# Zero-padded low keys for 128-row score products, and query and key weights split pair by pair on GpSimd

## The chip, the core and the metric

The kernel runs on one core of a Trainium2 chip. Its engines are TensorE (matmuls; loading weights is an instruction of its own beside them), VectorE, ScalarE, GpSimd and SyncE, which here issues the transfers (its queue is called SP). The metric is the time of one execution on the device in microseconds, less is better. Before the change it is 2414.99 us, the median of three runs (2414.29 to 2419.1).

## What is computed

A decoder layer on x of 8 sequences x 512 tokens x 512 features: self-attention with a router, cross-attention to a context of 77 tokens, and a feed-forward block over selected tokens. The change touches the self-attention alone, cut here to what matters:

```python
H, HD, W, G = 16, 64, 512, 128            # heads, head width, window, global tokens
h = rmsnorm(layernorm(x)) * norm_w        # (8, 512, 512)
q, k, v = (proj(w) for w in (w_q, w_k, w_v))   # each (8, 16, 512, 64)
ll = where(causal, q @ k.T * HD ** -0.5, NEG)
scores = h @ scorer_w + scorer_b          # a router: the 128 best tokens count twice
idx = top_k(scores, G)
lg = where(idx <= pos, q @ k[idx].T * HD ** -0.5, NEG)
attn = softmax(concat([ll, lg]))
o = attn[..., :W] @ v + attn[..., W:] @ v[idx]
return x + o @ w_out
```

As one window covers all 512 tokens, a selected token appears twice with the same score. The kernel therefore scores once, and counts the selected tokens' values twice.

## The kernel before

Matmuls run in a 32-bit type with rounded mantissa (F32R). To keep full precision each operand is split into a high part, rounded to that type, and a low part, the rest: a product is then high x high + low x high + high x low (`product`, three matmuls, L577 to L579). The weights of q, k and v lie in SBUF for the whole kernel, as `w_hi` and `w_lo`, each 128 x 4 x 1024. At the start they come in six pieces of 1024 KB (`W_ORDER`) through two halves of `o_t`: ScalarE rounds a piece (L368), VectorE subtracts (`split`, L477), and SP loads the next piece when a half is free.

A loop over the 8 sequences (`b`) does one batch after the other. Inside it the list `attention_plan()` sets the order, and each engine walks through the same list and does its own part: eight value projections ("v") with q and k of the first pair of heads among them, then 40 units ("s", 8 pairs x 5), then the last transposes and the output projection ("out"). A unit is one bank of 512 scores for one pair `p`, listed by `unit_blocks`: units 0 and 1 are one block of 512 keys (the last 128 queries of head 0 and of head 1), units 2 and 3 a block of 128 and one of 384, unit 4 two blocks of 256.

In step g TensorE makes the scores of unit g, the transposes of the probabilities of unit g-2 ("t", L673), the value products of unit g-3 ("pv", L688), and in units 0 and 2 the projection of q or k for the next pair ("q", "k", 12 matmuls). VectorE takes the maxima (L530, L525), copies the transposes to SBUF (L538), divides the outputs (L552, L553), and makes the low parts of q (L514) and k (L518). ScalarE makes the high parts (L392, L395, L396) and the exponentials (L405). The transposes of the outputs ("ot", L697) come at the end of a pair's unit 4, for the pair before. "t", "ot" and a few others take turns in two banks, `pt_bank`: each waits until the one before the last is copied out.

A score block is three matmuls into one bank: the high product over 128 rows (`q_both` holds 64 rows of high q and 64 of low q, `k_twice` the high k twice), the low product over 64 rows (high q x `k_lo`), and the causal mask in bf16 (`ident_b` x `causal_b`, L665):

```python
high = (q_both[:, p % 2, h, queries], k_twice[:, p % 2, h, 0:nk])
low = (q_both[rows, p % 2, h, queries], k_lo[rows, p % 2, 0:nk])
```

`rows` are the head's own 64 partitions. In unit 4 head 0 takes low first (L657, L659), and head 1 waits for that low product (`s_half`); elsewhere high comes first (L661, L664).

GpSimd makes the constants, the normalization of the next sequence in step 5 (`stats`, L325 to L339) and the residual of the output (L353). SP loads the next sequence at the start of a batch (L279) and moves the output's rows at its end (`results`).

Of the kernel before, what the change touches and what calls it, by code (L numbers as in the profile page):

```python
# [18 lines left out]
F32 = mybir.dt.float32  # L19
# [9 lines left out]
P = 128  # L29
# [97 lines left out]
def self_attention(nc, x, norm_w, w_q, w_k, w_v, w_out, scorer_w, scorer_b, x1):  # L127
# [3 lines left out]
    with ExitStack() as ctx:  # L131
# [9 lines left out]
        w_hi = {n: sb(f"w{n}_hi", [P, DC, H * HD], F32R) for n in "qkv"}  # L141
        w_lo = {n: sb(f"w{n}_lo", [P, DC, H * HD], F32R) for n in "qkv"}
# [7 lines left out]
        k_lo = sb("k_lo", [P, 2, S], F32R)  # L150
# [42 lines left out]
        s_ready, s_half = sem("s_ready"), sem("s_half")  # L193
# [10 lines left out]
        W_ORDER = [("v", 0), ("v", 1), ("q", 0), ("k", 0), ("q", 1), ("k", 1)]  # L204
        N_CONST = 9
# [41 lines left out]
        @block.sync  # L247
        def _(sp):
            sp.dma_start(xb[:, :, :], x_rows[0]).then_inc(x_in, 16)
            with nc.allow_non_contiguous_dma(reason="one column per chunk"):  # L250
                sp.dma_start(nw[:, :], norm_w.rearrange("(c p) -> p c", p=P)).then_inc(small_in, 16)
            sp.dma_start(sw[:, :], scorer_w.rearrange("d o -> o d").broadcast_to((P, D))).then_inc(small_in, 16)
            sp.dma_start(row_s[:, :], norm_w.rearrange("(o d) -> o d", o=1).broadcast_to((P, D))).then_inc(small_in, 16)
            sp.dma_start(sbias[:, :], scorer_b.rearrange("(o d) -> o d", o=1).broadcast_to((P, 1))
                         ).then_inc(small_in, 16)
            for i, (n, hw) in enumerate(W_ORDER):
                if i >= 2:
                    sp.wait_ge(split_lo, i - 1)
                sp.dma_start(o_t[:, DC * (i % 2):DC * (i % 2) + DC, :],
                             w_dram[n][:, :, 512 * hw:512 * hw + 512]).then_inc(w_loaded[i % 2], 16)  # L260
# [21 lines left out]
            sp.wait_ge(ht_lo_ready, DC * B)  # L282
            sp.dma_start(xb[:, :, :], x_rows[0]).then_inc(x_in, 16)
            results(B - 1)
            for half_done in x1_out:
                sp.wait_ge(half_done, 16 * B * TT // 2 + 1)

        @block.gpsimd
        def _(pl):
# [51 lines left out]

            stats(0)
            with pl.Fori(0, B) as b, done.loop(b, 14 + TT, B):
# [14 lines left out]
        def _(act):  # L358
# [6 lines left out]

            for i, (n, hw) in enumerate(W_ORDER):
                act.wait_ge(w_loaded[i % 2], 16 * (i // 2 + 1))
                nc.scalar.copy(w_hi[n][:, :, 512 * hw:512 * hw + 512],  # L368
                               o_t[:, DC * (i % 2):DC * (i % 2) + DC, :]).then_inc(split_hi, 1)
                if i == 1:  # L370
                    act.wait_ge(small_in, 64)
                    for c in range(DC):
                        normed(None, 0, c)
            act.wait_ge(split_lo, len(W_ORDER))
# [41 lines left out]
        def _(dv):  # L416
# [56 lines left out]
            def split(i):  # L473
                n, hw = W_ORDER[i]
                dv.wait_ge(split_hi, i + 1)
                cols = slice(512 * hw, 512 * hw + 512)
                nc.vector.tensor_tensor(w_lo[n][:, :, cols], o_t[:, DC * (i % 2):DC * (i % 2) + DC, :],  # L477
                                        w_hi[n][:, :, cols].bitcast(F32), ALU.subtract).then_inc(split_lo, 1)
# [14 lines left out]
            split(2)  # L493
            score_row(None, 0)
            split(3)
            for t in range(TT):
                rank(None, 0, t)
                if t in (1, 3):
                    split(4 + t // 2)
            with dv.Fori(0, B) as b, done.loop(b, 2 * TT + 2 * TT + 1 + NU, B):  # L500
                for kind, i in plan:
# [6 lines left out]
                    if kind in ("q_lo", "k_lo"):  # L508
                        slot, _ = pj(b, (kind[0], i))
                        dv.wait_ge(qk_hi, b * (2 * NPAIR) + 2 * i + (1 if kind == "q_lo" else 2))  # L510
                        for h in range(2):
# [5 lines left out]
                            else:  # L517
                                ins = nc.vector.tensor_tensor(k_lo[own, i % 2, :], pj_bank[slot][own, :],  # L518
# [55 lines left out]
        def _(pe):  # L574
# [46 lines left out]
            with pe.Fori(0, B) as b:  # L621
                for kind, i in plan:
                    if kind == "v":
# [7 lines left out]
                        for c in range(DC):  # L631
                            ins = product(pj_bank[slot][:, :], ht_hi[:, c, P * t:P * t + P], ht_lo[:, c, P * t:P * t + P],
                                          w_hi["v"][:, c, 512 * hw:512 * hw + 512],
                                          w_lo["v"][:, c, 512 * hw:512 * hw + 512], c == 0, c == DC - 1)
                        ins.then_inc(pj_ready, 1)
                    if kind in ("q", "k"):
                        slot, _ = pj(b, (kind, i))
                        pe.wait_ge(split_lo, 4 if i < NPAIR // 2 else 6)
                        pj_empty(b, (kind, i))
                        for c in range(DC):  # L640
                            ins = product(pj_bank[slot][:, :], w_hi[kind][:, c, P * i:P * i + P],
                                          w_lo[kind][:, c, P * i:P * i + P], ht_hi[:, c, :], ht_lo[:, c, :],
                                          c == 0, c == DC - 1)
                        ins.then_inc(pj_ready, 1)
                    if kind == "s":
# [6 lines left out]
                        for h, t, c0, nk in unit_blocks(u):  # L652
                            queries, rows = slice(P * t, P * t + P), head_rows(h)
                            high = (q_both[:, p % 2, h, queries], k_twice[:, p % 2, h, 0:nk])
                            low = (q_both[rows, p % 2, h, queries], k_lo[rows, p % 2, 0:nk])
                            if u == UNITS - 1 and h == 0:
                                nc.tensor.matmul(s_bank[slot][:, c0:c0 + nk], *low, start=True, stop=False  # L657
                                                 ).then_inc(s_half, 1)
                                nc.tensor.matmul(s_bank[slot][:, c0:c0 + nk], *high, start=False, stop=False)  # L659
                            else:  # L660
                                nc.tensor.matmul(s_bank[slot][:, c0:c0 + nk], *high, start=True, stop=False)  # L661
                                if u == UNITS - 1:
                                    pe.wait_ge(s_half, b * NPAIR + p + 1)
                                nc.tensor.matmul(s_bank[slot][:, c0:c0 + nk], *low, start=False, stop=False)  # L664
# [1097 lines left out]
```

## Time and profile before

| what | value |
|---|---|
| time, median of 3 runs | 2414.99 us |
| span of the profiled execution | 2414.0 us |
| self-attention, eight batches, one of them | 201.00 us |
| TensorE, VectorE, ScalarE, GpSimd busy in that batch | 197.31, 107.68, 71.46, 11.14 us |
| first stretch, to the first values | 48.70 us |
| cross-attention and feed-forward, from 1656 | 758.00 us |

The profile is of one execution; its span is the time from its first to its last recorded event, about 1 us less than the median of the runs. Times of matmuls overlap, since they are pipelined: the distance of two starts is the pace, not the duration that is printed. A granted clock of 1.00 stands for 2.4 GHz. "issue" as a releaser is time for which the profile shows no wait.

### The profile page before, as it was taken

How to read it: one execution, taken by the hardware profiler on the slowest of the kernel's cores; microseconds unless marked ns; L12 is line 12 of the kernel's file. 1: busy time of each engine (PE TensorE's matmuls, PEld its weight loads, DVE VectorE, ACT ScalarE, POOL GpSimd, SP SyncE). 2: the span in 40 equal slices, each digit the busy share in tenths (PEclk: the TensorE clock that was granted, in tenths of full speed). 3: DMA queues.
4: the chain of work that ended last, by engine and by line, in shares of the span. 5: the costliest groups of instructions: out<-in, count | busy, mean ns of one | idle time of the engine just before them, and what ended most of it. 6: DMA issues, size and time to landing. Idle time of an engine off the chain costs nothing. (4 is left out here: it accounts for less than half of the span.)

```text
span 2414.0 us, 35686 instructions
## 1 busy us (share of the span) xinstructions
PE 2241.6 (93%) x12029; PEld 1682.4 (70%) x12029; DVE 1349.6 (56%) x3145; ACT 845.5 (35%) x1541; POOL 429.2 (18%) x669
## 2 busy tenths in 40 slices
PE   3999999999999999999999999996898888878899
PEld 3786777678678677767767767773787888865543
DVE  4574376177257437617725743661787878845500
ACT  3442344144144234314414423441644444413210
POOL 2100000010010000001001000002866666620000
PEclk9999999999999999999999999997988888858999
DMA  5000000100100000010010000002013211141000
GB/s 183 1 1 31 23 1 10 45 1 1 54 1 1 31 23 1 10 45 1 1 54 1 1 28 27 1 10 91 29 56 102 83 55 55 53 152 50 1 0 18
DMA packets 46136, 80.23 MB, mean 33 GB/s; under 512 B 10067, under 2 KB 10067, under 8 KB 45448
## 3 DMA queue, kind: packets, MB, share of 16 engines
q1 hardware_dynamic: 45320, 75.85, 9.3%
q8 instruction: 103, 1.69, 0.3%
q0 software_dynamic: 640, 2.10, 0.2%
q14 instruction: 73, 0.60, 0.1%
HBM read 60.11 MB, written 17.83 MB: 32 GB/s over the span
## 5 line engine op out<-in xcount | busy, mean ns | idle before, releaser
L405 ACT ACTIVATE probs<-s_bank,nmax 128x512 f32<-128x512 f32 (+3 forms) x512 | 249.4, 525 | 421.6 <-DVE nmax L530 294.3
L530 DVE TENSOR_REDUCE nmax<-s_bank 128x1 f32<-128x512 f32 (+2 forms) x384 | 185.3, 510 | 305.7 <-PE s_bank L665 302.0
L688 PE MATMUL o_bank<-vals,probs_t 128*128 128x65 f32 x2560 | 322.2, 269 | 0.0
L688 PEld LDWEIGHTS o_bank<-vals,probs_t 128*128 128x128 f32 x2560 | 311.0, 192 | 1.4 <-DVE probs_t L538 1.4
L712 PE MATMUL pj_bank<-w_o,o_t 128*128 128x512 f32 x512 | 223.5, 597 | 6.0 <-ACT o_t L413 6.0
L538 DVE COPY probs_t<-pt_bank 128x512 f32<-128x512 f32 x320 | 218.0, 681 | 3.6 <-PE pt_bank L673 3.6
L319 POOL TENSOR_TENSOR idle<-ones 128x4 f32<-128x4 f32 x41 | 8.1, 198 | 1065.7 <-DMA probs<-in_x 1063.7
L673 PE MATMUL pt_bank<-ident,probs 128*128 128x128 f32 x1280 | 194.1, 274 | 0.0
L712 PEld LDWEIGHTS pj_bank<-w_o,o_t 128*128 128x128 f32 x512 | 97.2, 191 | 127.6 <-issue 127.6
L664 PE MATMUL s_bank<-k_lo,q_both 64*128 64x512 f32 (+3 forms) x448 | 184.9, 413 | 0.0
L514 DVE SCALAR_TENSOR_TENSOR q_both<-pj_bank,q_both 64x512 fp32r<-64x512 f32 x128 | 88.2, 689 | 141.6 <-ACT q_both L392 138.9
L661 PE MATMUL s_bank<-k_twice,q_both 128*128 128x512 f32 (+3 forms) x448 | 166.9, 373 | 0.0
L383 ACT ACTIVATE vals<-pj_bank,twice 128x512 f32<-128x512 f32 x64 | 43.9, 688 | 341.8 <-PE pj_bank L579 336.5
L1259 PEld LDWEIGHTS x_o_bank<-vx,p_t 77*128 77x128 f32 x1024 | 148.9, 224 | 17.2 <-issue 10.0
L1259 PE MATMUL x_o_bank<-vx,p_t 77*128 77x33 f32 x1024 | 143.8, 300 | 3.9 <-DVE att L1141 3.9
L570 DVE TENSOR_TENSOR probs<-pj_bank,probs 128x512 f32<-128x512 f32 x32 | 22.1, 692 | 213.8 <-PE pj_bank L712 195.3
L664 PEld LDWEIGHTS s_bank<-k_lo,q_both 64*128 64x128 f32 x448 | 81.9, 183 | 85.5 <-issue 72.1
L673 PEld LDWEIGHTS pt_bank<-ident,probs 128*128 128x128 f32 x1280 | 135.7, 141 | 0.0
L577 PE MATMUL pj_bank<-wv_hi,ht_hi 128*128 128x512 f32 x256 | 104.2, 407 | 22.9 <-ACT vals L383 9.9
L1245 PE MATMUL e_bank<-qk_bd,xl_t 128*128 128x308 f32 x256 | 96.9, 510 | 27.7 <-DVE e L1123 27.0
L1022 POOL TENSOR_TENSOR e<-e,fill 128x616 f32<-128x616 f32 x64 | 95.3, 1489 | 127.1 <-DVE fill L1129 126.9
L665 PE MATMUL s_bank<-causal_b,ident_b 128*128 128x128 bf16 x512 | 117.7, 230 | 0.0
(266 smaller groups left out, 4245.5 us busy)
## 6 DMA issues: line engine op xcount, KB each, us to landing
xb<-in_x SPq DMA_DIRECT2D x9, 1024.0 KB, 5.3
xt<-x SPq DMA_DIRECT2D x36, 256.0 KB, 2.8
probs<-in_x SPq DMA_DIRECT2D x32, 256.0 KB, 2.7
x<-probs SPq DMA_DIRECT2D x32, 256.0 KB, 2.0
am<-in_L_ffn_attention_mask SPq DMA_DIRECT2D x8, 1024.0 KB, 5.2
out<-x SPq DMA_DIRECT2D x32, 256.0 KB, 2.1
w_sb<-in_L_ffn_w SPq DMA_DIRECT2D x2, 4096.0 KB, 20.2
o_t<-in_L_attn_w_v SPq DMA_DIRECT2D x2, 1024.0 KB, 9.5
```

Source lines behind the costliest of these rows:

```text
L405: ins = nc.scalar.activation(probs[:, i % 2, c0:c0 + nk], s_bank[i % 2][:, c0:c0 + nk], ACT.Exp, bias=nmax[:, i % 4, n:n + 1])
L530: ins = nc.vector.tensor_reduce(nmax[:, i % 4, n:n + 1], s_bank[i % 2][:, c0:c0 + nk], AX.X, ALU.max, negate=True)
L538: nc.vector.tensor_copy(probs_t[:, i % 2, :], pt_bank[slot][:, :]).then_inc(ts_ready, 1)
L577: nc.tensor.matmul(out, lhs_hi, rhs_hi, start=start, stop=False)
L661: nc.tensor.matmul(s_bank[slot][:, c0:c0 + nk], *high, start=True, stop=False)
L664: nc.tensor.matmul(s_bank[slot][:, c0:c0 + nk], *low, start=False, stop=False)
L665: ins = nc.tensor.matmul(s_bank[slot][:, c0 + nk - P:c0 + nk], ident_b[:, :], causal_b[:, :], start=False, stop=True)
L673: ins = nc.tensor.transpose(pt_bank[slot][:, P * j:P * j + P], probs[:, i % 2, P * j:P * j + P], ident[:, :])
L688: ins = nc.tensor.matmul(o_bank[slot][:, o0:o0 + VW], probs_t[:, i % 2, c0 + P * kt:c0 + P * kt + P], vals[:, kt, 2 * p + h, :], start=(kt ...
L712: ins = nc.tensor.matmul(pj_bank[slot][:, :], o_t[:, c, P * i:P * i + P], w_o[:, c, :], start=(c == 0), stop=(c == NPAIR - 1))
L1245: ins = nc.tensor.matmul(e_bank[:, c, 0:CH * SK], xl_t[:, (i // 2) % 2, P * k:P * k + P], qk_bd[:, n.par, k].rearrange("p h k -> p (h k)") ...
L1259: ins = nc.tensor.matmul(o_bank[:, VX * h:VX * h + VX], p_t[:, i % 2, h // CH, P * (h % CH):P * (h % CH) + P], vx[:, n.par, 2 * CH * (i % ...
```

## The change

The low keys `k_lo` get a copy per head, in which the other head's 64 rows are zero; GpSimd writes the zeros once at the start. The low product then runs over all 128 rows with the same left operand as the high one: its low q meets zeros. The special order in unit 4 and its wait `s_half` go.

The weights of q and k are no longer kept. Per pair a slice of 128 columns of each is loaded (`w_raw`, 256 KB), GpSimd makes the high part by a multiplication by one and the low part by a subtraction (`split_slice`), after the projection that used the slice before is done, and the projection of the next pair waits for it (`w_made`). SP loads a slice when both splits of the one before are done (`next_slices`), ahead of the output's rows. The values' weights stay as they were. VectorE and ScalarE lose the four pieces of q and k at the start.

```diff
-        w_hi = {n: sb(f"w{n}_hi", [P, DC, H * HD], F32R) for n in "qkv"}
-        w_lo = {n: sb(f"w{n}_lo", [P, DC, H * HD], F32R) for n in "qkv"}
+        wv_hi, wv_lo = sb("wv_hi", [P, DC, H * HD], F32R), sb("wv_lo", [P, DC, H * HD], F32R)
+        w_raw = {n: sb(f"w{n}_raw", [P, DC, P]) for n in "qk"}
+        w_hi = {n: sb(f"w{n}_hi", [P, DC, P], F32R) for n in "qk"}
+        w_lo = {n: sb(f"w{n}_lo", [P, DC, P], F32R) for n in "qk"}
...
-        k_lo = sb("k_lo", [P, 2, S], F32R)
+        k_lo = sb("k_lo", [P, 2, 2, S], F32R)
...
+            def load_slices(i):
+                for n in "qk":
+                    sp.dma_start(w_raw[n][:, :, :], w_dram[n][:, :, P * i:P * i + P]).then_inc(raw_in[n], 16)
+            def next_slices(b):
+                for i in range(NPAIR):
+                    for n in "qk":
+                        sp.wait_ge(w_made[n], b * NPAIR + i + 1)
+                    load_slices((i + 1) % NPAIR)
+            load_slices(0)
...
             with sp.Fori(0, B - 1) as b:
+                sp.wait_ge(score_ready, b + 1)
                 sp.wait_ge(ht_lo_ready, b * DC + DC)
                 sp.dma_start(xb[:, :, :], x_rows[b + 1]).then_inc(x_in, 16)
+                next_slices(b)
                 results(b)
...
+            nc.gpsimd.memset(k_lo[:, :, :, :].bitcast(F32), 0.0).then_inc(const_made, 1)
...
+            def split_slice(n, count):
+                pl.wait_ge(raw_in[n], count * 16)
+                carry()
+                nc.gpsimd.tensor_scalar(w_hi[n][:, :, :], w_raw[n][:, :, :], 1.0, 1.0, ALU.mult, ALU.mult).then_inc(hi_made[n], 1)
+                pl.wait_ge(hi_made[n], count)
+                nc.gpsimd.tensor_tensor(w_lo[n][:, :, :], w_raw[n][:, :, :], w_hi[n][:, :, :].bitcast(F32),
+                                        ALU.subtract).then_inc(w_made[n], 1)
             stats(0)
+            for n in "qk":
+                split_slice(n, 1)
...
+                    if kind in ("q", "k"):
+                        pl.wait_ge(pj_ready, pj(b, (kind, i))[1])
+                        split_slice(kind, b * NPAIR + (i + 2))
...
-            split(2)
             score_row(None, 0)
-            split(3)
             for t in range(TT):
                 rank(None, 0, t)
-                if t in (1, 3):
-                    split(4 + t // 2)
...
-                                ins = nc.vector.tensor_tensor(k_lo[own, i % 2, :], pj_bank[slot][own, :],
+                                ins = nc.vector.tensor_tensor(k_lo[own, i % 2, h, :], pj_bank[slot][own, :],
...
-                        pe.wait_ge(split_lo, 4 if i < NPAIR // 2 else 6)
+                        pe.wait_ge(w_made[kind], b * NPAIR + i + 1)
...
-                            high = (q_both[:, p % 2, h, queries], k_twice[:, p % 2, h, 0:nk])
-                            low = (q_both[rows, p % 2, h, queries], k_lo[rows, p % 2, 0:nk])
-                            if u == UNITS - 1 and h == 0:
-                                nc.tensor.matmul(s_bank[slot][:, c0:c0 + nk], *low, start=True, stop=False
-                                                 ).then_inc(s_half, 1)
-                                nc.tensor.matmul(s_bank[slot][:, c0:c0 + nk], *high, start=False, stop=False)
...
+                            both = q_both[:, p % 2, h, P * t:P * t + P]
+                            nc.tensor.matmul(s_bank[slot][:, c0:c0 + nk], both, k_twice[:, p % 2, h, 0:nk],
+                                             start=True, stop=False)
+                            nc.tensor.matmul(s_bank[slot][:, c0:c0 + nk], both, k_lo[:, p % 2, h, 0:nk],
+                                             start=False, stop=False)
```

TensorE in unit 4 of the first pair, its order before (L657 and L664 are the low products, L659 and L661 the high ones):

```order
L657 MATMUL s_bank<-k_lo,q_both 128x256 [waits p_ready]
L659 MATMUL s_bank<-k_twice,q_both 128x256
L665 MATMUL s_bank<-causal_b,ident_b 128x128
L661 MATMUL s_bank<-k_twice,q_both 128x256
L664 MATMUL s_bank<-k_lo,q_both 128x256 [waits s_half]
L665 MATMUL s_bank<-causal_b,ident_b 128x128
L673 MATMUL pt_bank<-ident,probs 128x128 [waits ts_ready,p_ready]
```

The same place now (L681 is the high product, L683 the low one):

```order
L681 MATMUL s_bank<-k_twice,q_both 128x256 [waits p_ready]
L683 MATMUL s_bank<-k_lo,q_both 128x256
L685 MATMUL s_bank<-causal_b,ident_b 128x128
L681 MATMUL s_bank<-k_twice,q_both 128x256
L683 MATMUL s_bank<-k_lo,q_both 128x256
L685 MATMUL s_bank<-causal_b,ident_b 128x128
L693 MATMUL pt_bank<-ident,probs 128x128 [waits ts_ready,p_ready]
```

Head 0's two products have changed places, and no wait stands between the products any more; in the other units the order is what it was.

VectorE at the start, from the router scores to the factor of the values (`twice`), before:

```order
L440 TENSOR_SCALAR score<-score,sbias 128x4 [waits dve_step]
L477 TENSOR_TENSOR wq_lo<-o_t,wq_hi 128x4x512 [waits split_hi]
L446 COPY row_s<-pt_bank 128x512 [waits pt_ready]
L477 TENSOR_TENSOR wk_lo<-o_t,wk_hi 128x4x512 [waits split_hi]
L452 TENSOR_SCALAR junk,cnt<-row_s,score 128x512 [waits row_copied]
...
L463 TENSOR_SCALAR twice<-cnt 128x4 [waits dve_step]
L477 TENSOR_TENSOR wk_lo<-o_t,wk_hi 128x4x512 [waits split_hi]
```

And now:

```order
L473 TENSOR_SCALAR score<-score,sbias 128x4 [waits dve_step]
L479 COPY row_s<-pt_bank 128x512 [waits pt_ready]
L485 TENSOR_SCALAR junk,cnt<-row_s,score 128x512 [waits row_copied]
L488 SCALAR_TENSOR_TENSOR junk,cnt<-row_s,score,before 128x512 [waits dve_step]
L485 TENSOR_SCALAR junk,cnt<-row_s,score 128x512 [waits dve_step]
```

The subtractions for q and k are gone from VectorE (a third of the four stood among the rankings that are left out above). They stand on GpSimd now, in slices, behind the wait for the projection that used the slice before; this is the first of them in a batch:

```order
L363 ISA [waits pj_ready]
L338 TENSOR_TENSOR idle<-ones 128x4 [waits pool_step,raw_in_q]
L365 TENSOR_SCALAR wq_hi<-wq_raw 128x512
L367 TENSOR_TENSOR wq_lo<-wq_raw,wq_hi 128x512 [waits hi_made_q]
L382 REGISTER_ALU
```

## Rows read from the trace of the kernel before

**Rows 1.** A batch: stretch, length, busy PE PEld DVE ACT POOL, clock, DMA share, GB/s.
```profile
247.60:448.60 201.00, 197.31 (x1078) 146.98 (x1077) 107.68 (x254) 71.46 (x132) 11.14 (x26) 1.00 0.05 17
```

**Rows 2.** Timeline, TensorE, unit 1: start us, duration us, engine, line, operation, tiles.
```profile
384.53 0.39 PE L578 MATMUL pj_bank<-ht_hi,wq_lo 128*128 128x512 f32 x1
384.76 0.39 PE L579 MATMUL pj_bank<-ht_lo,wq_hi 128*128 128x512 f32 x1
384.98 0.39 PE L661 MATMUL s_bank<-k_twice,q_both 128*128 128x512 f32 x1
385.30 0.49 PE L664 MATMUL s_bank<-k_lo,q_both 64*128 64x512 f32 x1
385.73 0.23 PE L665 MATMUL s_bank<-causal_b,ident_b 128*128 128x128 bf16 x1
385.79 0.61 PE L673 MATMUL pt_bank<-ident,probs 128*128 128x128 f32 x4
```

**Rows 3.** Timeline, weight loads of the same unit; in brackets idle before and releaser.
```profile
384.76 0.19 PEld L661 LDWEIGHTS s_bank<-k_twice,q_both 128*128 128x128 f32 x1
385.30 0.18 PEld L664 LDWEIGHTS s_bank<-k_lo,q_both 64*128 64x128 f32 x1 [0.35 <-issue]
```

**Rows 4.** Timeline, TensorE, units 3 and 4, and the next pair's unit 3.
```profile
374.48 0.22 PE L661 MATMUL s_bank<-k_twice,q_both 128*128 128x128 f32 x1
...
375.71 0.61 PE L673 MATMUL pt_bank<-ident,probs 128*128 128x128 f32 x4
376.15 1.00 PE L688 MATMUL o_bank<-vals,probs_t 128*128 128x65 f32 x8
377.08 0.38 PE L657 MATMUL s_bank<-k_lo,q_both 64*128 64x256 f32 x1
377.39 0.39 PE L659 MATMUL s_bank<-k_twice,q_both 128*128 128x256 f32 x1
377.62 0.23 PE L665 MATMUL s_bank<-causal_b,ident_b 128*128 128x128 bf16 x1
...
378.33 0.61 PE L673 MATMUL pt_bank<-ident,probs 128*128 128x128 f32 x4
...
392.46 0.22 PE L661 MATMUL s_bank<-k_twice,q_both 128*128 128x128 f32 x1
```

**Rows 5.** Timeline, VectorE, ScalarE and TensorE from unit 3 to its transposes.
```profile
375.91 0.76 DVE L530 TENSOR_REDUCE nmax<-s_bank 128x1 f32<-128x128 f32 x2 [1.47 <-PE s_bank L665]
...
376.45 0.58 ACT L396 CAST k_twice<-pj_bank 64x512 fp32r<-64x512 f32 x1
...
377.62 1.38 DVE L518 TENSOR_TENSOR k_lo<-pj_bank,k_twice 64x512 fp32r<-64x512 f32 x2
...
379.04 0.69 DVE L525 TENSOR_REDUCE nmax<-s_bank 128x2 f32<-128x512 f32 x1
...
379.64 0.68 DVE L538 COPY probs_t<-pt_bank 128x512 f32<-128x512 f32 x1
...
380.88 0.60 PE L673 MATMUL pt_bank<-ident,probs 128*128 128x128 f32 x4
```

**Rows 6.** Timeline of the start: VectorE's last subtraction, TensorE's next value projection.
```profile
46.17 2.28 DVE L477 TENSOR_TENSOR wk_lo<-o_t,wk_hi 128x2048 fp32r<-128x2048 f32 x1
...
49.46 0.79 PE L577 MATMUL pj_bank<-wv_hi,ht_hi 128*128 128x512 f32 x1 [9.91 <-ACT vals L383]
...
50.05 0.63 PE L578 MATMUL pj_bank<-wv_hi,ht_lo 128*128 128x512 f32 x1
...
50.48 0.63 PE L579 MATMUL pj_bank<-wv_lo,ht_hi 128*128 128x512 f32 x1
```

**Rows 7.** GpSimd: L339 alone (count, ns min/median/max), and a subtraction's group (count, busy, mean ns).
```profile
L339 POOL TENSOR_SCALAR xb<-xb,st x36: 756/769/2797, 16.7 to 1510.2; 128x512 f32<-128x512 f32 x36
...
L1022 POOL TENSOR_TENSOR e<-e,fill 128x616 f32<-128x616 f32 x64 | 95.3, 1489 | 127.1 <-DVE fill L1129 126.9
```

**Rows 8.** Page, transfers by tile: count, KB each, median us to landing.
```profile
xb<-in_x SPq DMA_DIRECT2D x9, 1024.0 KB, 5.3
```

More of the change, by code:

```diff
@@ L192, in self_attention @@
         v_ready, v_sum_ready, qk_hi, qk_lo = sem("v_ready"), sem("v_sum_ready"), sem("qk_hi"), sem("qk_lo")
-        s_ready, s_half = sem("s_ready"), sem("s_half")
+        s_ready = sem("s_ready")
+        raw_in, hi_made, w_made = ({n: sem(f"{what}_{n}") for n in "qk"} for what in ("raw_in", "hi_made", "w_made"))
         max_ready, p_ready = sem("max_ready"), sem("p_ready")
@@ L203, in self_attention @@
         NPT0 = len(PT0)
[L204 to L205 removed]
+        N_CONST = 10
         assert NPJ % 2 == 0
@@ L255, in _ @@
                          ).then_inc(small_in, 16)
[L256 to L260, printed above, removed]
+            for hw in range(2):
+                sp.dma_start(o_t[:, DC * hw:DC * hw + DC, :],
+                             w_dram["v"][:, :, 512 * hw:512 * hw + 512]).then_inc(w_loaded[hw], 16)
+            def load_slices(i):
[7 more added lines that the diff above has]
+            load_slices(0)
             sp.dma_start(w_o[:, :, :], w_out.rearrange("(c p) d -> p c d", p=P)).then_inc(wo_in, 16)
@@ L340, in stats @@
                                             ALU.mult, ALU.add).then_inc(h_ready, 1)
+            def split_slice(n, count):
[5 more added lines that the diff above has]
+                                        ALU.subtract).then_inc(w_made[n], 1)
             stats(0)
-            with pl.Fori(0, B) as b, done.loop(b, 14 + TT, B):
+            for n in "qk":
+                split_slice(n, 1)
+            with pl.Fori(0, B) as b, done.loop(b, 14 + TT + 2 * NPAIR, B):
                 for r in range(2):
@@ L364, in normed @@
                                      scale=nw[:, c:c + 1]).then_inc(ht_hi_ready, 1)
[L366 to L374, printed above, removed]
+            for hw in range(2):
+                act.wait_ge(w_loaded[hw], 16)
+                nc.scalar.copy(wv_hi[:, :, 512 * hw:512 * hw + 512],
+                               o_t[:, DC * hw:DC * hw + DC, :]).then_inc(split_hi, 1)
+            act.wait_ge(small_in, 64)
+            for c in range(DC):
+                normed(None, 0, c)
+            act.wait_ge(split_lo, 2)
             with act.Fori(0, B) as b:
@@ L471, in normed, with split @@
                                                ALU.subtract).then_inc(ht_lo_ready, 1)
-            def split(i):
-                n, hw = W_ORDER[i]
-                dv.wait_ge(split_hi, i + 1)
+            def split(hw):
+                dv.wait_ge(split_hi, hw + 1)
                 cols = slice(512 * hw, 512 * hw + 512)
-                nc.vector.tensor_tensor(w_lo[n][:, :, cols], o_t[:, DC * (i % 2):DC * (i % 2) + DC, :],
-                                        w_hi[n][:, :, cols].bitcast(F32), ALU.subtract).then_inc(split_lo, 1)
+                nc.vector.tensor_tensor(wv_lo[:, :, cols], o_t[:, DC * hw:DC * hw + DC, :],
+                                        wv_hi[:, :, cols].bitcast(F32), ALU.subtract).then_inc(split_lo, 1)
             dv.wait_ge(const_made, N_CONST)
@@ L637, in _ @@
                         slot, _ = pj(b, (kind, i))
-                        pe.wait_ge(split_lo, 4 if i < NPAIR // 2 else 6)
+                        pe.wait_ge(w_made[kind], b * NPAIR + i + 1)
                         pj_empty(b, (kind, i))
                         for c in range(DC):
-                            ins = product(pj_bank[slot][:, :], w_hi[kind][:, c, P * i:P * i + P],
-                                          w_lo[kind][:, c, P * i:P * i + P], ht_hi[:, c, :], ht_lo[:, c, :],
+                            ins = product(pj_bank[slot][:, :], w_hi[kind][:, c, :], w_lo[kind][:, c, :], ht_hi[:, c, :], ht_lo[:, c, :],
                                           c == 0, c == DC - 1)
```

12 lines of the change are left out of this document (4 added, 8 removed).

## The prediction

> **What bounds the kernel now.** I read the stretches first: in one batch of the self-attention (201.00 us, eight of which make up two thirds of the span) TensorE is busy 197.31 us, VectorE 107.68, ScalarE 71.46 and GpSimd 11.14, at a granted clock of 1.00 [rows 1]. So TensorE sets the pace there and every other engine has slack on average. Then the timeline, to see what fills TensorE. One pair of heads runs from 374.48 to 392.46, 17.98 us [rows 4], without a gap; I call its five units u0 to u4 by the block they score. The projections, 128 rows high, follow one another at 0.23 us for 512 columns [rows 2]. The score products don't: the high product takes 0.32 us until the 64-row low product starts, and this one 0.43 until the causal product starts [rows 2]. The weight loads say why: the high product's load starts at 384.76, with the matmul ahead of it, and is hidden; the low product's load starts only with its own matmul at 385.30, after 0.35 us in which the load path stood idle with no releaser [rows 3]. So a change between 64 and 128 rows empties the array before it and before the next one, and lays one load open. Where a 128-row high product is followed by the 128-row causal one (377.39 to 377.62, 256 columns) there is 0.23 us, a load and its columns, and no such emptying [rows 4].
>
> **The score products, unit by unit.** The change keeps three products per block but makes all 128 rows high, in the order high, low, causal. I price the new ones by the 128-row pace: 0.23 us for 512 columns, by proportion 0.17 for 384 and 0.115 for 256, and never under 0.11, the pace of the four transposes from 375.71 to 376.15 [rows 4], which are bound by their loads. The causal product takes 0.06 until the next instruction [rows 2], and behind it I add 0.06, since its 128 columns can't cover a whole load.
> u0 and u1, one block of 512: before 0.81 (384.98 to 385.79) [rows 2], after 0.23 + 0.23 + 0.06 = 0.52; 0.29 less each.
> u2 and u3, blocks of 128 and 384: before 1.23 (374.48 to 375.71) [rows 4], after 0.11 + 0.11 + 0.06 + 0.06 + 0.17 + 0.17 + 0.06 = 0.74; 0.49 less each.
> u4, two blocks of 256: before 1.25 (377.08 to 378.33), and the eight value products ahead of it took 0.93 where eight loads at 0.11 make 0.88 [rows 4]. After 4 x 0.115 + 0.06 + 0.06 + 0.06 = 0.64; 0.61 + 0.05 = 0.66 less.
> A pair: 2 x 0.29 + 2 x 0.49 + 0.66 = 2.22 us, so 15.76 for 17.98. 64 pairs: 142 us.
>
> **A rule that speaks against it.** The row shows a 128-row load starting together with the 128-row matmul ahead of it, and a pace of 0.23 that has no room for an open load [rows 2, 3]. The Trainium skill, "TensorE: Matmul & The Clock Gate", section "The mechanism", says that a load overlaps matmuls in flight only where the row group differs, and elsewhere in it that the background weight buffer allows it too. By the first wording each low product, now in the same rows as the high one, would lay a load of 0.11 open: 512 blocks x 0.11 = 56 us of the gain lost. I go by the rows.
>
> **What is late next.** With TensorE 1.44 us earlier (0.49 + 0.66 + 0.29) at the transposes of u3, which stand in the next pair's u0, I follow the other chain, counted from the start of u3's scores (374.48 = 0). VectorE's maximum of u3 started at 1.43 (375.91) [rows 5] and now at 0.94. From there to the low keys it took 1.71 (377.62), now 2.65; ScalarE's last cast of the keys ends at 376.45 + 0.58, which is 2.55 and does not move, just ahead of it [rows 5]. Low keys 1.42 (to 379.04), the maximum of u4 0.60 (to 379.64), the copy 0.68: it ends at 5.35 [rows 5]. TensorE wants the bank that this copy empties for u3's transposes, since the transposes of the outputs lie between and there are two banks. It was there at 380.88, 6.40 [rows 5], and is now at 6.40 - 1.44 = 4.96. So a new wait of 0.4 us per pair, in the six pair changes of a batch that have output transposes ahead of them. Once a batch the copy of the router scores (a copy of 0.68) lies in that chain; I add 0.3. Bounds: none, if VectorE gets through a little sooner; 1 us a pair, if the GpSimd work slows this chain by a quarter of its own 2 us.
> A batch: 8 x 2.22 - 6 x 0.4 - 0.3 = 15.1 us. Eight batches: 121 us.
>
> **The weights.** Per pair GpSimd now makes two slices of 512 columns: a multiply at 0.77 us (the median of L339, 128x512) and a subtraction, for which L1022 (two operands, 616 columns, 1.49 us) gives 1.24 [rows 7], with a small instruction ahead: 2.2 us a slice, 4.4 a pair of 16. On an engine that was busy 11.14 of 201 us that costs nothing, if it stays beside TensorE: a slice is needed one pair later, some 13 us after the projection that frees it. Its transfers (two of 256 KB a pair, queued on SP behind the next batch's input and ahead of the results' rows) also have 10 us; 1024 KB landed in 5.3 us [rows 8]. TensorE's new wait for the split stands ahead of each projection; behind it are the next unit's scores, and VectorE and ScalarE after those. The cover is gone only if slice and transfer together take over 13 us.
> Does GpSimd slow VectorE? L339 took 0.77 us as a rule (the median of 36) and 2.80 once, beside VectorE's subtraction of two operands from SBUF at the start [rows 7]. The instructions of the chain above read PSUM and at most one operand from SBUF, unlike that subtraction, so I take nothing for them, and for the upper end the 1 us a pair named above. The Trainium skill, "SBUF — State Buffer", section "Who interferes with whom", says that a VectorE instruction with two SBUF inputs and a GpSimd one that reads SBUF block each other, and that a VectorE one with at most one such input does not contend outside the 2-port modes. The row agrees with the first half; no row here shows the second.
>
> **The start.** VectorE loses four subtractions of 2.28 us (one at 46.17), which stood between it and the factor that the first values wait for; TensorE waited 9.91 us there [rows 6]. Of the 9.1 us I take 8.5, since the first lay partly in a wait for the transposed scores. After the wait TensorE ran at the lower of its levels, 1.2 GHz: 0.43 us (50.05 to 50.48) for what takes 0.23 [rows 2, 6]; eight products x 0.2 = 1.6 us, which I count as won, an estimate, since a wait of only some 1.4 us is left. Against it, zeroing the low keys, 2048 columns, delays the constants: at most 4 x 0.77 = 3.1 us [rows 7], mostly under the first input's 5.3 us [rows 8]; I take 0.5. Start: 8.5 + 1.6 - 0.5 = 9.6 us.
>
> **Sum.** 121 + 9.6 = 130.6 us off the profiled span of 2414.0 gives 2283; the median of the runs lies 1.0 above the span, so 2284 us.
>
> **Rivals.**
> No wait appears: 64 x 2.22 + 9.6 = 152, 2263 us. For it: VectorE was idle 93 us of the batch [rows 1]. Against: the chain is a latency, not a load.
> The chain gets longer by GpSimd or by the work of ranking tokens on VectorE: 1 us a pair instead of 0.4 and a little in the others, some 40 us: 2325.
> Loads in the same rows don't overlap: 2284 + 56 = 2340. Against it rows 2 and 3.
> The change doesn't do what it says, since the emptying comes from something else that stays (such as two products into one bank): only the start is won, 2405. Against it the projections, which add into one bank at 0.23 [rows 2].
> On the other side: the weight slices come late. Place: TensorE's wait ahead of the key projection. A slice is loaded only after the split of the one before, so split + issue + transfer + split bound the pair. With 0.8 allowed for issuing that is 2.2 + 0.8 + 5.3 + 2.2 = 10.5 us [rows 7, 8]; it decides from 16.2, and the kernel is slower from some 18.1, where it costs 64 x 1 us for each us beyond. It needs a rounding to the 32-bit matmul type on GpSimd, or short packets, at about twice the price: at 20 us, 2530.
>
> **How the numbers follow.** My forecast, 2284 within 2265 to 2305: 0.52. No wait: 0.16. Longer chain: 0.15. Open loads: 0.05. Only the start: 0.05. Late slices: 0.04. The rest, 0.03, is what I haven't thought of, near no change. An error of 0.04 us in the price of a block moves 512 blocks by 20 us, which is the forecast's own width. The range reaches over the first three cases, 2250 to 2330, and leaves the rest. A measurement can tell 0.2%, some 5 us. Faster than that: all cases but the last two, 0.93; within it 0.03; slower 0.04.
>
> **What would show it.** Right: 128-row low products at 0.23 us behind the high ones, their loads starting with the high matmul; units 0.52, 0.74 and 0.64 us; a pair near 16.2 us; a wait of TensorE on the VectorE copy at u3's transposes; the first batch's wait of 9.91 us down to about 1.4. Wrong: an idle load path ahead of the low product, TensorE waiting ahead of a projection, VectorE's copies over 0.68 us, or a batch over 190 us.

## The result, and the profile after

The changed kernel takes 2291.06 us (median of 4 runs, 2289.59 to 2292.93) against 2416.53 us for the kernel before (4 runs, 2414.29 to 2419.1): a ratio of 0.948, with a 95% interval of 0.946 to 0.950. The prediction was 2284 us, with a range of 2250 to 2330. The profiled execution's span is 2287.9 us against 2414.0, 126.1 us less. Of the executions further below one, of the first kernel of the last experiment, took 7179.68 us, and that kernel's time is given without it. Where the 126.1 us went:

| stretch of the span | before | after | difference |
|---|---|---|---|
| to the first score product of batch 0 | 74.50 | 64.27 | -10.2 |
| one batch, clock at its full level | 201.0 | 187.1 | -13.9 |
| from there to the first input of the cross-attention (eight batches) | 1583.3 | 1474.9 | -108.4 |
| from there to the end (code that wasn't changed) | 756.2 | 748.7 | -7.4 |

The stretches of the changed kernel that answer to [rows 1]: start and end, length, busy time of TensorE, its weight loads, VectorE, ScalarE and GpSimd, granted clock, share of the transfers, GB/s. The first is a batch; the other two hold the start of the output projection of two batches.

```profile
412.70:599.80 187.10, 181.26 (x1078) 143.41 (x1077) 107.01 (x254) 71.44 (x132) 43.99 (x74) 1.00 0.13 40
...
376.00:391.00 15.00, 13.34 (x44) 6.80 (x43) 3.95 (x9) 2.65 (x4) 1.86 (x4) 0.89 0.10 35
565.00:578.00 13.00, 11.34 (x42) 6.01 (x41) 3.69 (x9) 2.65 (x4) 1.86 (x4) 1.00 0.11 38
```

TensorE loses 16.1 us of busy time a batch (197.31 to 181.26), the batch 13.9, so some 2 us came back as waiting. GpSimd goes from 11.14 to 43.99, VectorE and ScalarE stay. The last two lines explain most of why eight batches gave 108.4 and not 111: three of the eight output projections ran in part at the lower clock (0.89 as the mean of the stretch shown) and took 1.7 us longer (188.7 us a batch); before, it was one of eight.

Unit 1 on TensorE and its weight loads, the lines that answer to [rows 2, 3], and a pair's units 3 and 4, as in [rows 4]:

```profile
333.93 0.39 PE L607 MATMUL pj_bank<-ht_lo,wq_hi 128*128 128x512 f32 x1
333.93 0.19 PEld L681 LDWEIGHTS s_bank<-k_twice,q_both 128*128 128x128 f32 x1
334.15 0.39 PE L681 MATMUL s_bank<-k_twice,q_both 128*128 128x512 f32 x1
334.16 0.19 PEld L683 LDWEIGHTS s_bank<-k_lo,q_both 128*128 128x128 f32 x1
...
334.38 0.39 PE L683 MATMUL s_bank<-k_lo,q_both 128*128 128x512 f32 x1
...
334.61 0.10 PEld L685 LDWEIGHTS s_bank<-causal_b,ident_b 128*128 128x128 bf16 x1 [0.26 <-issue]
334.61 0.23 PE L685 MATMUL s_bank<-causal_b,ident_b 128*128 128x128 bf16 x1
...
334.68 0.61 PE L693 MATMUL pt_bank<-ident,probs 128*128 128x128 f32 x4
...
340.83 0.22 PE L681 MATMUL s_bank<-k_twice,q_both 128*128 128x128 f32 x1
...
341.55 0.60 PE L693 MATMUL pt_bank<-ident,probs 128*128 128x128 f32 x4
341.99 1.00 PE L708 MATMUL o_bank<-vals,probs_t 128*128 128x65 f32 x8
342.80 0.36 PE L681 MATMUL s_bank<-k_twice,q_both 128*128 128x256 f32 x1
343.00 0.28 PE L683 MATMUL s_bank<-k_lo,q_both 128*128 128x256 f32 x1
343.13 0.23 PE L685 MATMUL s_bank<-causal_b,ident_b 128*128 128x128 bf16 x1
343.17 0.36 PE L681 MATMUL s_bank<-k_twice,q_both 128*128 128x256 f32 x1
343.37 0.28 PE L683 MATMUL s_bank<-k_lo,q_both 128*128 128x256 f32 x1
343.49 0.23 PE L685 MATMUL s_bank<-causal_b,ident_b 128*128 128x128 bf16 x1
343.55 0.61 PE L693 MATMUL pt_bank<-ident,probs 128*128 128x128 f32 x4
```

High to low to causal product now goes at 0.23 and 0.23 us (before 0.32 and 0.43), and the low product's load starts at 334.16 with the high product ahead of it. An idle load path still stands ahead of the causal product (0.26 us with no releaser), and costs nothing that shows: the low product ahead of it goes at 0.23. Unit 1 takes 0.53, unit 3 (340.83 to 341.55) 0.72, unit 4 (342.80 to 343.55) 0.75.

The row of work that answers to [rows 5], on VectorE and TensorE, from the maximum of unit 3 to its transposes; in brackets the idle time ahead and what ended it:

```profile
341.75 0.75 DVE L558 TENSOR_REDUCE nmax<-s_bank 128x1 f32<-128x128 f32 x2 [0.43 <-PE s_bank L685]
...
343.46 1.38 DVE L546 TENSOR_TENSOR k_lo<-pj_bank,k_twice 64x512 fp32r<-64x512 f32 x2
344.87 0.69 DVE L553 TENSOR_REDUCE nmax<-s_bank 128x2 f32<-128x512 f32 x1
345.48 0.68 DVE L566 COPY probs_t<-pt_bank 128x512 f32<-128x512 f32 x1
...
345.75 0.23 PE L685 MATMUL s_bank<-causal_b,ident_b 128*128 128x128 bf16 x1
346.31 0.63 PE L693 MATMUL pt_bank<-ident,probs 128*128 128x128 f32 x4 [0.32 <-DVE probs_t L566]
```

From the causal product to the transposes it is 0.56 us here and 0.07 in unit 1: a wait of 0.49, which ends when VectorE's copy (345.48 + 0.68 = 346.16) has emptied the bank. The list of waits in one batch (us in total, times, longest) has it five times. It shows the idle time alone, 0.32 us where the matmul starts tell 0.49; one of the five is 0.54 there, 0.71 by the starts. Behind it stand the start's lines on TensorE that answer to [rows 6]:

```profile
PE pt_bank L693 <- DVE probs_t L566: 1.8, 5, 0.5
```
```profile
40.92 0.50 PE L605 MATMUL pj_bank<-wv_hi,ht_hi 128*128 128x512 f32 x1 [1.07 <-ACT vals L416]
41.26 0.39 PE L606 MATMUL pj_bank<-wv_hi,ht_lo 128*128 128x512 f32 x1
```

The first wait of 9.91 us is 1.07, and behind the first product (0.34 us to the next) they go at 0.23 us, at a granted clock of 1.00 from 40.92 to 44 and without the stretch at the lower of the two levels.

### The profile page after: what moved, and what is told of

Read it like the earlier page. It is cut to its first block and busy times, and to the rows that moved or that the text cites. A ratio compares the mean times of both kernels' runs of the same rounds, so it can differ in the third digit from the quotient of the medians.

```text
span 2287.9 us, 36708 instructions
## 1 busy us (share of the span) xinstructions
PE 2112.8 (92%) x12029; PEld 1651.3 (72%) x12029; DVE 1333.4 (58%) x3141; ACT 837.5 (37%) x1537; POOL 697.9 (31%) x1060
## 2 busy tenths in 40 slices
DMA packets 112665, 110.13 MB, mean 48 GB/s; under 512 B 12083, under 2 KB 78643, under 8 KB 111976
## 5 line engine op out<-in xcount | busy, mean ns | idle before, releaser
L338 POOL TENSOR_TENSOR idle<-ones 128x4 f32<-128x4 f32 x171 | 36.1, 211 | 1129.8 <-PE pj_bank L607 812.2
L681 PE MATMUL s_bank<-k_twice,q_both 128*128 128x512 f32 (+3 forms) x512 | 189.5, 372 | 0.0
L683 PE MATMUL s_bank<-k_lo,q_both 128*128 128x512 f32 (+3 forms) x512 | 163.9, 320 | 0.0
L425 ACT ACTIVATE q_both<-pj_bank 64x512 fp32r<-64x512 f32 x128 | 75.7, 592 | 103.0 <-PE pj_bank L607 102.2
```

What stands on the lines that cost most here:

```text
L681: nc.tensor.matmul(s_bank[slot][:, c0:c0 + nk], both, k_twice[:, p % 2, h, 0:nk], start=True, stop=False)
L683: nc.tensor.matmul(s_bank[slot][:, c0:c0 + nk], both, k_lo[:, p % 2, h, 0:nk], start=False, stop=False)
```

## The experiments

**One half alone: the weights.** The 64-row low products and their old order go back in:

```diff
+    rows = head_rows(h)
-    matmul(..., both, k_lo[:, p % 2, h, 0:nk], ...)
+    matmul(..., q_both[rows, p % 2, h, queries], k_lo[rows, p % 2, h, 0:nk], ...)
```

> The changed kernel with its score products put back to 64 low rows (and the old order in the last unit); weight slices, GpSimd's splits and the shorter start stay. My theory: a batch costs what it did before, 201.0 us, since slices and splits hide under TensorE; only the start is about 10 us shorter, so about 2405 us (2399 if the 7.4 us that the cross-attention and the last stages lost come with the weights). Rival A, that slices or splits cost or gain something in the batch: a batch off 201.0 by more than 0.5 us, which is 4 us of the time. Rival B, that half of the gain comes from the weights' placement and not from the rows: a batch under 195.

2402.01 us, ratio 0.994 (0.993 to 0.996); a batch of 200.95 us, TensorE's busy time as before, GpSimd's as after:

```profile
440.20:641.15 200.95, 197.28 (x1077) 147.08 (x1076) 107.72 (x254) 71.30 (x132) 43.91 (x74) 1.00 0.12 37
```

So slices and splits are free in the batch, and the start alone is worth some 10 us (the first input of the cross-attention is issued at 1647.15, 10.7 us earlier than before).

**The other half alone: the scores.**

```diff
-    k_lo = sb("k_lo", [P, 2, S], F32R)
+    k_lo = sb("k_lo", [P, 2, 2, S], F32R)      # 4 KB a partition more; zeroed by GpSimd
-    w_o = sb("w_o", [P, NPAIR, D])              # and its load
+    w_o = w_lo["v"] viewed as [P, NPAIR, D]
```

> The kernel before with the 128-row low products and padded low keys alone; q and k weights stay resident. To make room, the output projection multiplies with the value weights' low parts in place of its own weights, which are not loaded (that part of the output is wrong; shapes and types are the same). My theory: a batch of 187.0 us as in the changed kernel, the start as before plus about 1.8 us for the larger fill of zeros, so 2416 - 8 x 14.0 + 2 = 2306 us (2299 if the later stages' 7.4 us come with the rows). Rival A (the splits by GpSimd slow something inside the batch): a batch below 186.5. Rival B (part of the batch gain comes from the slices): a batch above 188.

2297.92 us, ratio 0.951 (0.950 to 0.953).

```profile
423.50:610.20 186.70, 181.09 (x1077) 143.40 (x1076) 106.99 (x255) 71.31 (x132) 11.14 (x26) 1.00 0.06 18
```

The batch gains what the whole change gains, with GpSimd at its old 11.14 us. The two halves add up: 12.6 us (2414.60 to 2402.01) and 116.7 (to 2297.92) make 129, against the 125.5 of the whole change (123.5 if that is counted from 2414.60 too); the executions of each kernel scatter by 3 to 7 us, so the difference isn't clear of noise. The batch is 0.3 us shorter than with the slices. One wait (485.63 in the changed kernel) is 0.54 with them and 0.33 here, the longer one behind a VectorE gap of 0.23 us that the trace gives no releaser for; it isn't the slices, as the next run shows.

**No slices in the loop.**

```diff
-    pl.wait_ge(pj_ready, pj(b, (kind, i))[1])
-    split_slice(kind, b * NPAIR + (i + 2))
-    next_slices(b)                               # SP's loads
```

> The changed kernel without the weight slices in the loop: no loads and no splits after the first pair's, whose weights all pairs use (the output of the other pairs is wrong). It takes away 2.1 us of GpSimd work per slice and 30 MB of transfers. My theory: they hide, 2291 us within 4, a batch of 187.0 as with them. Rival A (GpSimd's work slows VectorE's, or the transfers take something from TensorE): faster by over 5 us. Rival B (the slices cause the lower clock in the output projection of three batches): those 1.7 us each are gone, 2286 us.

2291.17 us, against 2291.06 with them; a batch of 187.03 with GpSimd back at 11.14. Nothing of the 33 us of GpSimd work a batch and of the 33.6 MB of transfers (110.13 MB in the profile with them, 76.56 without; I had written 30) is on the path of a batch. Rival A is out. Rival B isn't borne out in the time, but isn't excluded: this profile has one slow output projection and not three, and two of 1.7 us are within the scatter of the executions. The three profiles without slices have one slow projection of eight each, the eight with slices have one to four. What lowers the clock there stays open.

**A quarter of the products.** 128 rows in units 0 and 1 only:

```diff
+    rows = slice(0, P) if u < 2 else head_rows(h)
```

> The changed kernel with 128-row low products in units 0 and 1 alone (two of a pair's eight low products), 64 rows and the old order in units 2 to 4. My theory (every change between 64 and 128 rows costs, and a low product's load that had nothing to hide under is hidden): units 0 and 1 give their 0.28 us each, 8 x 0.56 = 4.5 us a batch, 196.5 us, 64 x 0.56 = 36 us against the kernel with the weights alone, so 2366 us, and no new wait at the bank. Rival A, every low product gives the same quarter of a quarter (2 of 8 of the 14 us): 197.5 us a batch, 2374. Rival B, as long as one unit still changes rows the cost stays: 201, 2402.

2366.81 us, ratio 0.980 (0.978 to 0.981), on the forecast of 2366.

```profile
1024.69:1221.29 196.60, 192.91 (x1077) 146.57 (x1076) 107.44 (x254) 71.31 (x132) 43.90 (x74) 1.00 0.12 38
```

4.35 us a batch off the 200.95, for 16 blocks: 0.27 us a block, which is unit 1's own 0.81 less 0.53. The cost belongs to each block whose low product has 64 rows, and no part of the gain waits for the last such block to be gone (rival B). A share by count would have been 3.5 us (rival A). No wait for the bank is in this kernel's list: TensorE isn't early enough yet.

**The new wait.** The transposes of the attention output one unit earlier, so that unit 3's transposes get a bank that ScalarE empties:

```diff
-    if g >= 9 and (g - 9) % UNITS == 0 and (g - 9) // UNITS < NPAIR - 1:
-        plan.append(("ot", (g - 9) // UNITS))
+    if g >= 8 and (g - 8) % UNITS == 0 and (g - 8) // UNITS < NPAIR - 1:
+        plan.append(("ot", (g - 8) // UNITS))
```

> The changed kernel with one line of the plan moved: the transposes of a pair's attention output stand one unit earlier (unit 3 in place of unit 4), so that the transposes of unit 3's exponentials take the bank that ScalarE frees early and not the one that VectorE's copy of unit 2 frees. My theory (TensorE's new wait is that bank, at the end of VectorE's row of low keys, maxima and copy): the wait of 0.49 us in six pair changes of eight batches goes, 8 x 6 x 0.49 = 23 us, a batch of 184.1 us, 2268 us. Rival A (the row on VectorE is late anyway and TensorE waits one step on, for the copied exponentials or the maximum): 2285 to 2292. Rival B (the early transposes wait for the normalised output): slower, over 2295.

2275.06 us, ratio 0.942 (0.940 to 0.943), and a batch of 185.53: 1.5 us less, where I had expected 2.9. The five waits are gone, but the sixth pair change has a longer one; first the list of waits, then the timeline of VectorE and TensorE there:

```profile
PE pt_bank L693 <- DVE row_s L479: 1.2, 1, 1.2
```
```profile
682.39 0.68 DVE L566 COPY probs_t<-pt_bank 128x512 f32<-128x512 f32 x1
...
683.44 1.38 DVE L546 TENSOR_TENSOR k_lo<-pj_bank,k_twice 64x512 fp32r<-64x512 f32 x2
684.85 0.69 DVE L479 COPY row_s<-pt_bank 128x512 f32<-128x512 f32 x1
...
685.68 0.63 PE L693 MATMUL pt_bank<-ident,probs 128*128 128x128 f32 x4 [1.16 <-DVE row_s L479]
```

The router scores' transposes take a bank between the pairs' own, so here the bank of VectorE's copy of the score row (684.85 + 0.69) comes next. Four waits of 0.49 and one of 0.71 less 0.84 more at the sixth (0.32 to 1.16) make 1.8 us. Where the 0.71 was, the value products now wait 0.25 us for the next copy of the same row (at 670.30, seen on the weight loads), which leaves 1.6, the measured 1.5. The place of the wait was right; I had counted six banks of one kind where there are five and one.

**Does VectorE's row set it?** One more VectorE instruction (a 64x512 subtraction into a tile that nothing reads), on the row and off it:

```diff
     ins.then_inc(qk_lo, 1)
+    if kind == "k_lo":        # the other kernel: "q_lo"
+        nc.vector.tensor_tensor(extra[:, :], sw[0:HD, :], sw[0:HD, :], ALU.subtract)
```

> The changed kernel with one more VectorE instruction of about 0.65 us (a 64x512 subtraction into a tile that nothing reads) right behind the low keys of each next pair, ahead of the maximum of the last unit. My theory: it stands in the row of VectorE's work that TensorE's wait for the bank hangs on, so each of the five to six waits of a batch is 0.65 us longer: 26 to 31 us, 2317 to 2322 us. Rival, the wait is set elsewhere (by the exponentials, or by TensorE's own order): below 2300.

> The same instruction behind the low queries two units earlier, where VectorE has about 1.8 us of idle time before the next maximum. My theory: off the row, so nothing: 2289 to 2295 us. Rival, any VectorE work costs (it is 57% busy but in a chain all the way): 2317 or more, as with the other place.

2335.48 us (0.967, 0.966 to 0.969) and 2305.16 us (0.954, 0.953 to 0.955): 44 and 14 us more than the changed kernel. The difference between the places, 30 us, is what I expected of the first alone; that the second costs 14 I had not expected. The waits for the copy in a batch, of the first kernel and the second:

```profile
PE pt_bank L696 <- DVE probs_t L569: 5.8, 5, 1.5
PE pt_bank L720 <- DVE row_s L480: 1.0, 1, 1.0
...
PE o_bank L711 <- DVE probs_t L569: 0.7, 1, 0.7
```
```profile
PE pt_bank L696 <- DVE probs_t L569: 2.2, 5, 0.5
...
PE s_bank L684 <- DVE k_lo L547: 0.4, 1, 0.4
```

In the second kernel, a later pair's low keys and its first score product behind them:

```profile
709.63 1.39 DVE L547 TENSOR_TENSOR k_lo<-pj_bank,k_twice 64x512 fp32r<-64x512 f32 x2 [0.23 <-issue]
...
711.15 0.49 PE L684 MATMUL s_bank<-k_twice,q_both 128*128 128x512 f32 x1
```

On the row, a wait that was 0.32 is 1.02: five of the six grow by the instruction's 0.70, and one by 1.20 (0.30 to 1.49), since the instruction itself takes 1.18 there (the last section has it). A wait of 0.70 stands at the value products of the second pair, where the changed kernel has one of 0.26 that its list doesn't show. Off the row, the instruction delays the first pair's low keys by 0.4 us, where no pair ahead hides them, and those of the later pair shown, which end at 711.02 and hold its first score product back by another 0.4. Three of the five waits of a batch are 0.54, two more than in the changed kernel; at both, token ranking follows the added instruction and VectorE comes to unit 3's maximum late (1.31 us after its scores begin, not 0.92). That is 0.4 + 0.4 + 2 x 0.22 = 1.2 of the batch's 1.4 us (188.4); the rest I haven't traced. The rival (any VectorE work costs) is right for a third of it: the place decides the other two.

**A version that beats both.** The transposes of the output in unit 3, and those of the score row one unit earlier, so that its copy is out of the way:

```diff
-    if g == 18:
+    if g == 17:
         plan.append(("score", 0))
```

The first kernel has a third move, the value weights' low parts at the start by GpSimd instead of VectorE; the second has not.

> The kernel with the earlier transposes of the attention output, and two more moves: the score rows' transposes one unit earlier (TensorE's 1.16 us wait for the bank that VectorE's copy of the score row frees, once a batch), and at the start the value weights' low parts by GpSimd behind its statistics and not by VectorE (GpSimd's 0.2 us steps took 2.3 and 2.2 us beside VectorE's two subtractions). My theory: 8 x 1.16 = 9 us less and some 4 us at the start, against 2275: 2262 us; a batch of 184.4. Rival A, the score rows then wait for the score itself, or the wait only moves: a batch of 185.5, 2271. Rival B, GpSimd's two large subtractions (5 us each) come later than TensorE's first product of the values: the start is no shorter, 2266.

> The changed kernel with the transposes of the attention output in unit 3 and those of the score rows one unit earlier; the start as in the changed kernel. My theory (GpSimd's two large subtractions made the start 1.9 us longer, since VectorE's score products ran beside them at 1.14 to 3.18 us in place of 0.69; the move of the score rows is worth 1.6 us a batch by itself): a batch of 183.9 us, the first copy of the doubled factors at 39.8 us, 2268.6 - 1.9 = 2266.7 us. Rival (the earlier low parts helped elsewhere at the start, such as the first pair's weights): 2268 to 2271.

2268.36 us (2268.57 with the execution named at the result; 0.939, 0.937 to 0.941) and 2264.94 us (0.938, 0.936 to 0.940). In both no wait of TensorE for those banks is left; a batch is 183.84 and 184.2 us, in place of 185.5. The third move did not pay: the first factor for the values is ready at 41.67 us with it and at 40.50 without (I had expected 39.8). GpSimd's steps did lose their 4 us, but then its own subtractions ran beside VectorE's score products:

```profile
18.07 8.99 POOL L374 TENSOR_TENSOR wv_lo<-o_t,wv_hi 128x2048 fp32r<-128x2048 f32 x2
...
24.46 3.18 DVE L475 CUSTOM_DVE_ANT_0 junk<-xb,sw 128x512 bf16<-128x512 f32 x1
...
27.68 1.14 DVE L475 CUSTOM_DVE_ANT_0 junk<-xb,sw 128x512 bf16<-128x512 f32 x1
```

Those products take 0.69 us otherwise. The two medians can't be told apart by their intervals; the profile of the start decides for the version without. It is 1.1% faster than the changed kernel, and 6.2% than the one before.

## Why the prediction was right, step by step

**The score products: right in sum.** The pair was to take 15.76 us without the wait, and took 16.25 with one of 0.49 in it: 15.76. Unit 1 was priced at 0.52 and took 0.53. Units 2 and 3 were priced at 0.74 and took 0.80 and 0.72. I had taken units 0 and 2 for twins of units 1 and 3; they were dearer before (0.90 and 1.32, not 0.81 and 1.23) and are now (0.62 and 0.80), so that their gains, 0.28 and 0.52, came out. Unit 4 was too cheap, 0.64 against 0.75: I had let its high products go at their columns' pace, 0.115, and they took 0.20. Each stands behind a short product, and the low product's load starts 0.08 us behind the high product (343.25 behind 343.17, 342.88 behind 342.80) and not with it. The value products ahead of it made up for most of that: 0.81 where I had counted 0.88.

**The rule on loads.** The low product's load starts 0.01 us behind the high matmul and is over before that ends, in the same 128 rows; before, the 64-row load stood open [rows 3]. By the one wording of the Trainium skill, "TensorE: Matmul & The Clock Gate", section "The mechanism", an overlap needs another row group; this trace disagrees, and the 56 us of that rival didn't come. What does cost is a 64-row product among 128-row ones, 0.27 us a block: 0.09 ahead of it and 0.20 from it to the next (0.32 and 0.43 against 0.23). That each of the two changes of rows empties the array is my reading of the gaps; the runs show only the price. No run has two 64-row products in a row, so how much of the 0.20 is the change, and how much the 64-row product itself, stays open.

**The new wait: right in place, 0.49 for 0.4.** The row of VectorE's work came out nearly to the hundredth: from the start of unit 3 its copy was to end at 5.35 and ended at 5.33 (340.83 to 346.16). TensorE came at 4.99, 0.03 later than I had it. The transposes start 0.15 behind the copy's end, which I had left out: 5.33 + 0.15 - 4.99 = 0.49. The two VectorE runs show that the row sets it. For the whole batch: 15.1 us predicted, 13.9 measured. Six waits of 0.49, 0.22 more in one of them behind VectorE's gap, and one that I had at nothing make 3.4 us where I had counted 2.7. The one left out is in the second pair: its value products come 0.26 us late, held by the next copy of VectorE's row. TensorE's list of waits doesn't have it, since the trace counts next to none of it as idle time of its matmuls; the weight loads show it:

```profile
640.22 0.97 PEld L708 LDWEIGHTS o_bank<-vals,probs_t 128*128 128x128 f32 x8 [0.24 <-DVE probs_t L566]
```

That is 0.7 of the 1.2. The other 0.4 or so are the products: with three moves, where no wait for a bank is left, a batch of 183.84 is 17.2 us shorter than before, 17.4 without that 0.26, and 8 x 2.22 is 17.8; the first pair alone gained 2.09.

**GpSimd and the slices: right.** 0.62 and 1.27 us an instruction (0.77 and 1.24 predicted), no TensorE wait for a split in the list, and 2291.17 us without them. VectorE's instructions beside them keep their means: the low keys 684 ns before and 686 after, the copy 681 and 681.

```profile
L546 DVE TENSOR_TENSOR k_lo<-pj_bank,k_twice 64x512 fp32r<-64x512 f32 x16 | 11.0, 686 | 2.8 <-ACT k_twice L429 2.5 <-issue 0.2
L566 DVE COPY probs_t<-pt_bank 128x512 f32<-128x512 f32 x40 | 27.2, 681 | 0.5 <-PE pt_bank L693 0.5
```

The Trainium skill, "SBUF — State Buffer", section "Who interferes with whom", says that a VectorE instruction with at most one operand from SBUF, outside the 2-port modes, doesn't contend with GpSimd. No row of before showed that; these agree. Its other half, two operands, is in the last section's lines.

**The start: right, 10.2 for 9.6.** The wait shrank to 1.07 (I had 1.4) and the lower clock went with it. The larger fill with zeros cost more than I took (VectorE's first instruction at 6.13 us instead of 4.39), but its statistics only moved from 6.14 to 6.36, since they wait for the input.

**What I didn't have.** Two more slow output projections than before (3.4 us), and the last 7.4 us. These lie in code that is the same in both kernels. In eleven profiles of kernels that share it, this part takes from 748.2 to 756.2 us; the kernel before is the highest. Followed matmul by matmul (3401 in each), 3.8 of the 7.4 us lie in one stretch of 173 matmuls, here of before and of after:

```profile
2161.34:2226.30 64.96, 54.64 (x173) 29.64 (x171) 35.08 (x80) 25.79 (x56) 8.01 (x8) 0.87 0.30 115
```
```profile
2038.66:2099.79 61.13, 50.81 (x173) 26.19 (x172) 34.93 (x80) 25.79 (x56) 7.91 (x8) 0.94 0.32 121
```

That is a lower granted clock in one execution, not the change: in the kernel with the weights alone and in the one with the earlier transposes, the same stretch takes 65.0 us. The other 4.0 us are lost in the 500 us ahead of it, with as much time at the lower clock in both. There the two kernels that keep the weights of q and k in SBUF take 502.8 and 503.5 us, and the nine others 496.1 to 499.9; so this part may come with the weights, and why stays open.

Without the 7.4 us the profiled span would have been 2295, 12 us over the 2283 predicted: 9 from the batches' 15.1, 3.4 from the clock at the output projection, 0.6 back at the start. That 2284 came so close is in part luck: 7.4 us in which no step of the forecast had a part made up for more than half of what the batches fell short.

## What to carry to other kernels

In a chain of matmuls that TensorE bounds, a product over half the rows among full-height ones can cost more than it saves: padding it with zeros to full height took 0.27 us off each block. The price shows in the pace, 0.32 and 0.43 us for what takes 0.23; an idle load path with no releaser points to it but doesn't prove it, since the causal product's load has one that costs nothing. When such a saving moves TensorE ahead, write out the other engines' row from one shared buffer to the next; here it gave the new wait at the bank to a tenth of a microsecond and left out a smaller one in the second pair, and who empties the buffer could then be changed by a line of the plan. When a change needs room and buys it with transfers and an idle engine's work, run each half alone: it shows which half is the gain and that the other costs the batch nothing.

## What the runs showed of the hardware that was not expected

GpSimd and VectorE hold each other up in both directions when VectorE reads two operands from SBUF. At the start of the changed kernel two steps of GpSimd on 128x4 elements, 0.20 us otherwise, lasted as long as VectorE's subtraction beside them:

```profile
13.93 2.29 DVE L509 TENSOR_TENSOR wv_lo<-o_t,wv_hi 128x2048 fp32r<-128x2048 f32 x1 [4.01 <-ACT wv_hi L402]
13.95 2.33 POOL L353 TENSOR_TENSOR res_next<-st,ones 128x4 f32<-128x4 f32 x1
...
16.60 2.29 DVE L509 TENSOR_TENSOR wv_lo<-o_t,wv_hi 128x2048 fp32r<-128x2048 f32 x1 [0.37 <-ACT wv_hi L402]
16.73 2.22 POOL L338 TENSOR_TENSOR idle<-ones 128x4 f32<-128x4 f32 x1 [0.17 <-POOL res_next L354]
```

And the added VectorE subtraction, 0.68 us as a rule, took 1.18 where GpSimd's rounding of a slice (from 476.81, 0.61 us) ran, while the subtraction of that slice behind it took 1.58 us instead of 1.27:

```profile
476.77 1.18 DVE L551 TENSOR_TENSOR extra<-sw 64x512 f32<-64x512 f32 x1
```
```profile
477.50 1.58 POOL L368 TENSOR_TENSOR wk_lo<-wk_raw,wk_hi 128x512 fp32r<-128x512 f32 x1
```
